# A graph layer with 64 graphs: x's sums and splits moved to the head of a step, the masks moved, one product kept in PSUM, weight splits taken apart

## The reference

```python
mask = (adj[None] == labels[:, None, None, None]).astype(dt)
weight = mask / (jnp.sum(mask, axis=-1, keepdims=True) + EPS)
agg = jnp.einsum('dbmn,bnh->bmdh', weight, hid).reshape(..., D * H)
out = relu(_linear(agg, Wd, bd))
r = sigmoid(_linear(out, Wri, bri) + _linear(hid, Wrh, brh))
z = sigmoid(_linear(out, Wzi, bzi) + _linear(hid, Wzh, bzh))
n = tanh(_linear(out, Wni, bni) + r * _linear(hid, Wnh, bnh))
out = (1.0 - z) * n + z * hid
# layer norm over the features, times gamma, plus beta
```

## Time and profile before

| | us |
|---|---|
| runs of the kernel before | 563.91, 565.45, 566.31 (median 565.45) |
| the profiled execution's own time | 564.8 |
| its span, from the first to the last instruction | 563.0 |

### The profile page before, as it was taken

One profiled execution on the slowest core, in us unless ns is written; L12 is line 12 of the kernel. 1 busy time (PEld: TensorE's weight loads), 2 busy tenths in 40 slices (PEclk: granted clock), 3 DMA queues, 4 the chain that ended last, 5 costly groups with the idle time before them and its releaser, 6 DMA issues.

```text
span 563.0 us, 10619 instructions
## 1 busy us (share of the span) xinstructions
PE 515.1 (91%) x3011; PEld 463.0 (82%) x3011; DVE 485.7 (86%) x1071; ACT 389.7 (69%) x746; POOL 319.5 (57%) x339
## 2 busy tenths in 40 slices
PE   4569999999999999999999999999999999999980
PEld 2458988888898888888988888898888889888860
DVE  3985788999898899899988999988898999998765
ACT  4656777677776767777777677777767677776751
POOL 3865455566655556665555556655556665554343
PEclk9989999999999999999999999999999999999995
DMA  8211011221211111111122121102122120200100
GB/s 288 94 48 48 10 58 66 67 66 48 66 39 47 65 65 65 47 65 47 37 65 65 65 65 47 56 28 65 65 65 65 47 65 27 75 28 29 40 37 37
DMA packets 19877, 33.42 MB, mean 59 GB/s; under 512 B 2224, under 2 KB 6576, under 8 KB 19856
## 3 DMA queue, kind: packets, MB, share of 16 engines
q1 hardware_dynamic: 19728, 32.78, 18.0%
q0 software_dynamic: 128, 0.39, 0.2%
HBM read 24.77 MB, written 8.39 MB: 59 GB/s over the span
## 4 chain that ended last, share of the span: by engine, by line
PE 86%; issue 5%; POOL 3%; DVE 3%; ACT 2%; DMA 1%; POOLq 0%; DVEq 0%; SPq 0%; ACTq 0%
PE y_bank L278 32%; PE alpha L278 23%; PE p_bank L341 12%; PE gamma L278 11%; PE beta L278 6%; PE t_bank L381 3%; POOL wo_lo L812 1%; PE t_bank L322 1%; DMA shared<-in_wdT 1%; POOL shared L783 0%; POOL o_lo L818 0%; POOL shared L788 0%; DVE y_lo L572 0%; ACT y_hi L437 0%; ACT wo_hi L517 0%
## 5 line engine op out<-in xcount | busy, mean ns | idle before, releaser
L776 POOL TENSOR_TENSOR x_lo<-x_f,x_hi 128x512 fp32r<-128x512 f32 x31 | 40.5, 1305 | 123.3 <-ACT x_hi L419 123.3
L278 PE MATMUL y_bank<-wd_hi,x_hi 128*128 128x512 f32 x256 | 104.8, 409 | 4.8 <-DVE wd_lo L560 4.8
L437 ACT ACTIVATE y_hi<-y_bank 128x512 fp32r<-128x512 f32 x128 | 76.2, 595 | 46.9 <-PE y_bank L278 45.5
L278 PE MATMUL y_bank<-wd_lo,x_hi 128*128 128x512 f32 x256 | 102.3, 400 | 0.0
L278 PE MATMUL y_bank<-wd_hi,x_lo 128*128 128x512 f32 x256 | 102.1, 399 | 0.0
L572 DVE TENSOR_TENSOR y_lo<-y_bank,y_hi 128x512 fp32r<-128x512 f32 x128 | 86.8, 678 | 11.2 <-ACT y_hi L437 11.1
L341 PE MATMUL p_bank<-y_hi,masks 128*128 128x256 f32 x256 | 69.1, 292 | 18.4 <-issue 13.2
L445 ACT ACTIVATE p_bank<-p_bank,ratio 128x256 f32<-128x256 f32 x128 | 52.6, 457 | 31.2 <-PE p_bank L341 31.2
L783 POOL TENSOR_TENSOR shared<-x_rows,shared 128x512 f32<-128x512 f32 x32 | 41.2, 1287 | 57.8 <-ACT shared L482 57.8
L341 PEld LDWEIGHTS p_bank<-y_hi,masks 128*128 128x128 f32 x256 | 48.5, 190 | 27.6 <-issue 27.3
L341 PE MATMUL p_bank<-y_lo,masks 128*128 128x256 f32 x256 | 66.7, 283 | 0.0
(11 more groups left out here) (119 smaller groups left out, 1422.3 us busy)
## 6 DMA issues: line engine op xcount, KB each, us to landing
x_f<-in_xT SPq DMA_DIRECT2D x32, 256.0 KB, 2.6
x_rows<-in_x SPq DMA_DIRECT2D x32, 256.0 KB, 3.0
out<-shared SPq DMA_DIRECT2D x32, 256.0 KB, 2.0
adj_in<-in_adjT SPq DMA_DIRECT2D x31, 128.0 KB, 2.4
shared<-in_wgT SPq DMA_DIRECT2D x2, 576.0 KB, 7.1
shared<-in_wdT SPq DMA_DIRECT2D x3, 256.0 KB, 5.7
vec_rows<-in_vectors SPq DMA_DIRECT2D x1, 512.0 KB, 8.0
x_rows<-in_vectors SPq DMA_DIRECT2D x1, 512.0 KB, 9.4
```

The lines of the kernel that those rows point to most:

```text
L278: done = nc.tensor.matmul(dst, m, w, start=(first and t == 0), stop=(last and t == 2), skip_group_check=inside)
L437: nc.scalar.activation(y_hi[:, g, half(b)], y_bank[b][:, :], ACT.Copy)\
L776: nc.gpsimd.tensor_tensor(*split_lo(x_lo[:, (i + 1) % XRING, 0:4, :], x_f[:, (i + 1) % 2, 0:4, :], x_hi[:, (i + 1) % XRING, 0:4, :])).then ...
```

## The change

It does five things.

1. x. The four sums of x of pair i + 1 move from the middle of POOL's step to its head, ahead of the split. ACT then converts all eight blocks in one instruction of 1024 elements, where it converted four; the second conversion ahead of y_high(1, 1) goes. POOL splits all eight in one. In step 0 the sums of pair 0 and their split stand ahead of the steps. SP's load_x waits for that one split.
2. Masks. From step 2 on, DVE makes the masks of pair i + 1 right behind y_low(0, 0); in steps 0 and 1 behind y_low(1, 0).
3. Counts. The three instructions on the counts stand at the head of the next step, between those of the norm.
4. n's product with r goes into the PSUM bank `mix` in place of an SBUF tile, and pre_n reads it there.
5. The gate weights are split block by block, over steps 0 to 2, in the order of their use (`ASKED`); the lo parts of wx on DVE, those of wo on POOL.

```diff
+ASKED = (B11, T1, T2, B21, T3, T4, B22)
 # SP
-                    sp.wait_ge(xsum_ready, up(3 * i + 3, 3))
+                    if i == 0:
+                        sp.wait_ge(xlo0_ready, 1)
+                        sp.wait_ge(xslo0_ready, 1)
+                    else:
+                        sp.wait_ge(xlo_ready, up(i))
                     load_x(i, up(i + 2))
 # PE, product
+                    if q == 0:
+                        pe.wait_ge(wx_ready, ASKED.index(w) + 1)
                     three_passes(dst[:, 0:GATE], ...)
-                    if q == 0 and w <= B22:
-                        pe.wait_ge(wo_plain_ready, 1)
-                    elif q == 0:
-                        pe.wait_ge(wo_sums_ready, w - B22)
+                    if q == 0:
+                        pe.wait_ge(wo_ready, ASKED.index(w) + 1)
 # ACT, step
                 y_high(0, 0)
                 if i == 1:
-                    act.wait_ge(wx_sum, 4)
-                    nc.scalar.activation(wx_hi[:, T1:B12, :], wx_f[:, T1:B12, :], ACT.Copy).then_inc(wx_hi_ready, 1)
+                    weights_x(T2)
+                    weights_o(B11)
+                if i == 2:
+                    weights_x(B22)
+                    weights_o(T3)
...
                 if has_pair(i + 1):
-                    split_plain(i + 1, ...)
+                    k = i + 1
+                    act.wait_ge(xsum_ready, up(3 * k + 3, 3))
+                    if k >= XRING:
+                        act.wait_ge(p3_done, up(i - 2))
+                    nc.scalar.activation(x_hi[:, k % XRING, :, :], x_f[:, k % 2, :, :], ACT.Copy).then_inc(xhi_ready, 1)
                 y_high(0, 1)
...
-                for k in (0, 1) if i == 0 else (i + 1,):
-                    if has_pair(k):
-                        act.wait_ge(xsum_ready, up(3 * k + 3, 3))
-                        ...
-                        nc.scalar.activation(x_hi[:, k % XRING, 4:8, :], x_f[:, k % 2, 4:8, :], ACT.Copy)\
-                            .then_inc(xshi_ready, 1)
                 y_high(1, 1)
 # DVE, step
+                if has_pair(i):
+                    count_add(i)
+                if has_pair(j):
+                    norm_centre(0)
+                if has_pair(i):
+                    count_invert(i)
+                if has_pair(j):
+                    norm_centre(1)
+                if has_pair(i):
+                    count_ratio(i)
...
                 y_low(0, 0)
...
+                if has_pair(i + 1) and i >= 2:
+                    make_masks()
                 if has_pair(i - 1):
                     sum_labels(i - 1, 1)
+                if i == 1:
+                    weights_x(T1)
+                if i == 2:
+                    weights_x(T3)
                 if has_pair(m):
                     dve.wait_ge(rz_ready, up(m + 1))
                     if m >= 1:
                         dve.wait_ge(pre_ready, up(m))
-                    nc.vector.tensor_tensor(rn_sb[:, :]..., c_sb[:, :, :, 0:128], rz_sb[...], ALU.mult)
+                        dve.wait_ge(result_ready, up(2 * m, 2))
+                    nc.vector.tensor_tensor(mix[:, :]..., c_sb[:, :, :, 0:128], rz_sb[...], ALU.mult)
...
-                                            rn_sb[:, :].rearrange("p (g j f) -> p g j f", g=2, j=2),
+                                            mix[:, :].rearrange("p (g j f) -> p g j f", g=2, j=2),
                                             c_sb[:, :, :, GATE:512], ALU.add).then_inc(pre_ready, 1)
                 y_low(0, 1)
-                if i == 0:
-                    invert_counts(0)
...
-                if has_pair(i + 1):
-                    dve.wait_ge(adj_loaded[(i + 1) % 2], ...)
-                    if i >= 1:
-                        dve.wait_ge(p_done, up(2 * i, 2))
-                    for d in range(D):
-                        nc.vector.tensor_scalar(*label_masks(i + 1, d)).then_inc(masks_ready, 1)
                 if has_pair(m):
                     dve.wait_ge(zpart_ready, up(m + 1))
...
                 y_low(1, 0)
+                if i < 2:
+                    make_masks()
...
-                if has_pair(i + 1):
-                    invert_counts(i + 1)
 # POOL, ahead of the steps and in a step
+            sum_blocks(0, lambda n, k=1: n, 16)
+            pool.wait_ge(xshi0_ready, 1)
+            nc.gpsimd.tensor_tensor(*split_lo(x_lo[:, 0, 4:8, :], ...)).then_inc(xslo0_ready, 1)
...
                 if has_pair(i + 1):
-                    pool.wait_ge(xhi_ready, up(i + 2))
-                    nc.gpsimd.tensor_tensor(*split_lo(x_lo[:, (i + 1) % XRING, 0:4, :], ...)).then_inc(xlo_ready, 1)
+                    k = i + 1
+                    sum_blocks(k, up, up(16 * (k // 2 + 1), 8))
+                    pool.wait_ge(xhi_ready, up(k + 1))
+                    nc.gpsimd.tensor_tensor(*split_lo(x_lo[:, k % XRING, :, :], ...)).then_inc(xlo_ready, 1)
+                if i == 1:
+                    for w in (B11, T1, T2):
+                        weights_o(w)
+                if i == 2:
+                    for w in (B21, T3, T4, B22):
+                        weights_o(w)
                 if has_pair(m):
                     pool.wait_ge(tanh_ready, up(m + 1))
...
-                for k in (0, 1) if i == 0 else (i + 1,):
-                    if has_pair(k):
-                        sum_blocks(k)
-                for k in (0, 1) if i == 0 else (i + 1,):
-                    if has_pair(k):
-                        split_sums(k)
```

More of the change, by code:

```diff
@@ L89, in later @@
             return shared[:, at:at + parts * 512]
[L91 to L94, removed]
+        u2_sb, u3_sb = later(0, 1), later(512, 1)
+        c_sb = later(1024, 4).rearrange("p (g j f) -> p g j f", g=2, j=2)
+        rz_sb = later(3072, 2).rearrange("p (g j f) -> p g j f", g=2, j=2)
         pre_n = later(4096, 1)
@@ L413, in _ @@
         def _(act):
[L414 to L420, removed]
             act.wait_ge(ident_zero, 1)
             nc.scalar.activation(warm[:, :], power[:, 0:1], ACT.Sigmoid)
-            split_plain(0, None, 16)
+            act.wait_ge(x_loaded[0], 16)
+            nc.scalar.activation(x_hi[:, 0, 0:4, :], x_f[:, 0, 0:4, :], ACT.Copy).then_inc(xhi_ready, 1)
             for b in range(2):
@@ L429, in _, with weights_x, weights_o @@
                         .then_inc(wd_hi_ready, 1)
+            act.wait_ge(xsum_ready, 3)
+            nc.scalar.activation(x_hi[:, 0, 4:8, :], x_f[:, 0, 4:8, :], ACT.Copy).then_inc(xshi0_ready, 1)
             def step(i, up):
                 q, m = i - LAG_GATES, i - LAG_MIX
+                def weights_x(w):
+                    if w <= B22:
+                        act.wait_ge(wx_loaded, 32)
+                    else:
+                        act.wait_ge(wx_sum, 4)
+                    nc.scalar.activation(wx_hi[:, w, :], wx_f[:, w, :], ACT.Copy).then_inc(wx_hi_ready, 1)
+                def weights_o(w):
+                    if w <= B22:
+                        act.wait_ge(wo_loaded, 32)
+                    else:
+                        act.wait_ge(wo_sum, 4)
+                    nc.scalar.activation(wo_hi[:, w, :], wo_f[:, w, :], ACT.Copy).then_inc(wo_hi_ready, 1)
                 def y_high(g, b):
@@ L483, in step @@
                 if i == 1:
-                    act.wait_ge(wo_loaded, 32)
-                    nc.scalar.activation(wo_hi[:, 0:PLAIN, :], wo_f[:, 0:PLAIN, :], ACT.Copy).then_inc(wo_hi_ready, 1)
+                    weights_o(T1)
+                    weights_x(B21)
+                if i == 2:
+                    weights_o(T4)
                 if has_pair(i - 1):
@@ L769, in split_sums, with weights_o @@
-                def split_sums(k):
-                    pool.wait_ge(xshi_ready, up(k + 1))
-                    nc.gpsimd.tensor_tensor(*split_lo(x_lo[:, k % XRING, 4:8, :], x_f[:, k % 2, 4:8, :],
-                                                      x_hi[:, k % XRING, 4:8, :])).then_inc(xslo_ready, 1)
-                if has_pair(i + 1):
-                    pool.wait_ge(xhi_ready, up(i + 2))
-                    nc.gpsimd.tensor_tensor(*split_lo(x_lo[:, (i + 1) % XRING, 0:4, :], x_f[:, (i + 1) % 2, 0:4, :],
-                                                      x_hi[:, (i + 1) % XRING, 0:4, :])).then_inc(xlo_ready, 1)
+                def weights_o(w):
+                    pool.wait_ge(wo_hi_ready, ASKED.index(w) + 1)
+                    nc.gpsimd.tensor_tensor(*split_lo(wo_lo[:, w, :], wo_f[:, w, :], wo_hi[:, w, :])).then_inc(wo_ready, 1)
@@ new lines, in step @@
+                if has_pair(i + 1):
+                    k = i + 1
+                    sum_blocks(k, up, up(16 * (k // 2 + 1), 8))
+                    pool.wait_ge(xhi_ready, up(k + 1))
+                    nc.gpsimd.tensor_tensor(*split_lo(x_lo[:, k % XRING, :, :], x_f[:, k % 2, :, :],
+                                                      x_hi[:, k % XRING, :, :])).then_inc(xlo_ready, 1)
+                if i == 1:
+                    for w in (B11, T1, T2):
```

(6 more changed lines are left out.)

122 lines of the change are left out of this document (66 added, 56 removed).

## The result

The changed kernel takes 547.95 us (547.56 to 548.57), beside 565.02 us (563.91 to 566.31) for the kernel before on the same chip: a ratio of 0.970, 95% interval 0.968 to 0.971. It is faster by 3.0%. The time lies inside the range, 3 us above the 545 that was said. The profiled execution took 547.88 us, of which 546.1 are span: 16.9 less than the 563.0 before.

What follows compares the result with a forecast made beforehand. PE, busy 91% of the span, was taken as the bound, with a repeated stall to remove. 563.0 - 19.9 (steady steps) - 0.4 (opening) = 542.7 span; plus 1.8 and 0.65 gives 545.1, said as 545; range 540.5 to 557, own range 541 to 549.

Steps and rivals of the forecast that it cites:

- (a): Head of VectorE's step: norm and count instructions, the ratio meeting GpSimd's sums; y_low(0, 0) at frame 2.7 us.
- (b): Masks on VectorE behind y_low(0, 0): start at frame 3.2 to 3.35, take 0.8 us, end at 4.0 to 4.15.
- (c): n's product on VectorE starts at frame 4.9 to 5.05; pre_n, with one SBUF input, takes 0.67 us, ends at 6.3.
- (d): x's conversion on ACT, eight blocks in one behind the sigmoid: frame 4.2 to 5.25, at no cost.
- (e): GpSimd's eight-block split from frame 5.3 to 7.9, z_part to 10.6; y_low(1, 1) starts at 13.7, slack 0.5 us.
- (f): SP's loads: load_x waits for the pair's split, adjacency needed 6 us earlier; both land a step ahead, no cost.
- first rival: n's product loses to GpSimd's split in each step: 1.8 us a step, 595 us in all, slower; chance 0.10.
- second rival: The product loses to the split only in some 6 steps, after the loop's branches: 556 us; chance 0.12.
- the third: Rival: a smaller wait, 0.1 to 0.4 us a step, at y_low(1, 1) or the transposes: 548 to 556; chance 0.12.
- the stall: PE's wait before p_part(i, 1, False) for y_low(1, 1), steps 3 to 30; 0.71 us a step was to go.
- the race: Whether VectorE's product starts before GpSimd's x split, the first holding the other; predicted margin 0.25 to 0.4 us.
- The opening: Steps 0 to 2, ending at 56.37 us before the change; forecast -0.4 us, bounds -2.5 and +2.5.

## Why the prediction was right, and the term that was off

**The steady step.** Every part of it came out within 0.25 us, as the rows above show (start of step 15 is 246.45). (a) y_low(0, 0) ran from 2.47; I had said 2.7, and the ratio did stand beside a sum, 0.63. (b) Masks from 3.28, in 0.90; sum_labels ended at 5.08, said 5.1. (c) The product started at 5.00 (said 4.9 to 5.05), and pre_n ended at 6.42 (6.3). (d) x's conversion ran from 4.17 to 5.22 (4.2 to 5.25). (e) The split ran from 5.30 to 7.96 (7.9), z_part ended at 10.59 (10.6), y_low(1, 1) started at 13.68 (13.7). (f) No wait of PE is for a load. The step is 15.564 where 15.59 was forecast, so 20.5 us went instead of 19.9.

The walk also named the right danger. Margin and price of the first rival are measured now: 0.30 us, and 1.81 us in each step lost. The second rival, that the steps at the start of the loop lose, didn't occur: these steps have the product at 4.93 and keep their 15.56. Nor did the third, a smaller wait in the stall's place: no step loses 0.1 us.

**What the walk didn't tell** is how the gain divides. It treated the parts as one. The runs give the product in PSUM 0.59 of 0.73 us, and leave 0.14 for masks, x and counts together. One by one: the masks' move costs 0.15 without the fused split (it loses the race), and it gives 0.04 with it. That the rest of the 0.14 comes from the fused conversion and split, and from the counts at the head, follows by subtraction only; they weren't tried alone.

**The opening.** Here the term was -0.4, within -2.5 and +2.5, and it measured +3.3, outside its bounds. It makes up 3.7 of the difference; the steady steps give 0.6 back and the drain adds 0.3: 3.4 in the profiled execution, and the medians differ by 2.95. The sum came within its range because the room above 545, 4 us, was a little more than this miss; the sum's large term, 19.9, is what was right.

The walk was wrong in all three steps.

- Step 0: step 1 was to start at +2 to +3, and started at +4.4. The masks of pair 0 took 2.78 us for 0.89, PE's first p_bank came 1.5 us late, and a part of the matmuls behind it ran at the low clock: from PE's first y matmul to step 1 it was 17.49 us, and 16.84 with the clock full. How the rest divides isn't shown.
- Step 1: the transposes were to come level and step 2 at -0.4, so this step was to win 2.4 to 3.4 us. It won 0.8, and step 2 started at +3.6. The walk counted the 4.13 us before the transposes as time to be won, and they did go: the transposes have no wait in the kernel after. But the masks of pair 2 took their place, 2.77 us beside POOL's splits of weights and of o's sums, and PE stood 1.02 us and then 4.53 us at the next p_banks. I had given these masks their place in the order, and not the price that the earlier trace rows show for them beside POOL.
- Step 2 was to win 0.8 and won 0.3.

The clock isn't the miss. The prediction had 1 us more for it. It cost 2.4 us in the kernel after and 1 to 2 us in the old opening, so 0.4 to 1.4 us more.

Two readings in the prediction are off by less than 0.1 us and change nothing: frame 6.71 is 6.70 by its rows, and "about 3.05" is 2.97 by the two rows that it names. Its chances add up to 0.99, and it gives two ranges, 541 to 549 and 540.5 to 557; the time lies in both.

## What to carry to other kernels

Where VectorE stands beside GpSimd, look at which operands lie in SBUF: putting one intermediate into PSUM was a small edit here and gave four fifths of the steady gain, and all the reordering gave the rest, and lost it again in the opening. When two instructions exclude each other, work out who asks first and by how much, because the price isn't gradual: 0.1 us on the wrong side cost 1.8 us a step. And a new order for the steady state needn't be used while the pipeline fills: walk the opening apart, with the contended prices, and keep the old order there if it is better.

## What the runs showed of the hardware

Masks have a single input in SBUF (128x256, int32 to fp32r), and they are held beside GpSimd as well: four take 0.89 to 0.90 alone and 1.70 to 2.78 beside it in the rows shown. The operations that read one operand from PSUM and one from SBUF weren't held: y_low took 0.67 to 0.69 in each of its 128 executions in all thirteen traces, and pre_n 0.69 in each of 32 in the eleven kernels that have the product in PSUM. That is no more than the product with both inputs in SBUF when undisturbed (0.69). Of two operations that exclude each other, the one whose recorded start is 0.1 us later was held, and at 0.04 us either could be. A wait that is short can be dear through the clock: 48 matmuls took 12.39 us in a window with idle stretches of 1.61 us and, just before it, of 2.42 us, and zero matmuls in PE's idle time, whose results nobody reads, made the whole kernel 2.6 us faster by the medians.
